# The first two tiles of a mixture-of-experts kernel taken from fixed rows, loaded while attention still runs

## What is computed

```
h  = layernorm(x)
theta, phi, g = projections of ctx, h, h to 128 channels
p  = softmax(theta @ phi)                      # 512 x 512, per batch
t  = p @ g;  t = relu(layernorm over both axes (t) * gamma + beta)
x  = x + out_w @ t + out_b + ctx               # attention
n  = layernorm(x);  w = softmax(n @ gate_w.T)  # 32 experts
w  = the 8 largest of w per token, divided by their sum
x  = x + sum over the 8 experts e of w[e] * (silu(n @ w_gate[e]) * (n @ w_up[e])) @ w_down[e]
```

## Time and profile before

| what | us |
|---|---|
| median of 3 runs | 759.28 |
| lowest, highest | 755.08, 759.33 |
| span of the profiled execution | 758.7 |

### The profile page before, as it was taken

One profiled execution on the slowest core, in us unless ns is written; L12 is line 12 of the kernel. 1 busy time (PEld: TensorE's weight loads), 2 busy tenths in 40 slices (PEclk: granted clock), 3 DMA queues, 4 the chain that ended last, 5 costly groups with the idle time before them and its releaser, 6 DMA issues.

```text
span 758.7 us, 24265 instructions
## 1 busy us (share of the span) xinstructions
PE 708.8 (93%) x3682; PEld 584.4 (77%) x3683; DVE 566.7 (75%) x1355; ACT 434.8 (57%) x1047; POOL 380.1 (50%) x297
## 2 busy tenths in 40 slices
PE   7999999988788799999999999999999999999994
PEld 5466555656667688889988999889988889888993
DVE  4578888878655488677877878877887778767882
ACT  1775666662035366556666666666667566656662
POOL 2006777767776434443544544434553455444554
PEclk9999999999799999999999999999999999999997
DMA  8996777587898999999999999999999999999995
GB/s 297 361 335 234 261 269 288 215 289 273 291 299 188 184 211 224 218 202 237 215 225 240 225 211 238 224 251 228 244 236 245 211 229 248 243 210 227 220 155 79
DMA packets 174405, 179.85 MB, mean 237 GB/s; under 512 B 36864, under 2 KB 128768, under 8 KB 174368
## 3 DMA queue, kind: packets, MB, share of 16 engines
q0 software_dynamic: 30976, 73.48, 43.0%
q1 hardware_dynamic: 118240, 67.67, 35.1%
q10 hardware_dynamic: 25152, 38.30, 15.6%
HBM read 92.25 MB, written 87.13 MB: 236 GB/s over the span
## 4 chain that ended last, share of the span: by engine, by line
SPq 38%; PE 23%; issue 18%; DMA 7%; POOL 7%; ACT 4%; DVE 2%; ACTq 1%; DVEq 1%; POOLq 0%
SPq L320 23%; SPq L325 8%; POOL x_sorted L512 6%; SPq L439 5%; PE bank L1532 3%; PE bank L1533 3%; PE bank L1539 3%; DMA x_sorted<-xn_kept,slots 3%; DMA x_all<-x_sorted 2%; PE bank L1325 2%; DMA x_sorted<-prob,last_slots 1%; PE bank L1504 1%; ACT prob L670 1%; PE bank L1505 1%; PE bank L1506 1%
## 5 line engine op out<-in xcount | busy, mean ns | idle before, releaser
L569 POOL DMA_INDIRECT out_dram<-ctx_all,x_all x144 | 243.2, 1689 | 276.7 <-issue 131.5
L1532 PE MATMUL bank<-gu_hi,xT_hi 128*128 x576 | 194.7, 338 | 2.1 <-ACT xT_hi L800 1.2
L1533 PE MATMUL bank<-gu_lo,xT_hi 128*128 x576 | 195.6, 340 | 0.0
L813 ACT ACTIVATE ctx_all<-bank 128x512 f32<-128x512 f32 x144 | 86.0, 597 | 104.9 <-issue 78.9
L512 POOL DMA_INDIRECT x_sorted<-xn_kept,slots x96 | 100.0, 1042 | 86.7 <-issue 82.0
L1539 PE MATMUL bank<-gu_hi,xT_lo 128*128 x576 | 137.9, 361 | 0.0
L1208 DVE STREAM_TRANSPOSE x_all<-x_all 128x512 f32<-128x512 f32 x146 | 103.9, 712 | 26.5 <-DMA x_all<-x_sorted 22.2
L1255 DVE SCALAR_TENSOR_TENSOR probT<-probT,x_all,bank 128x192 f32<-128x192 f32 x144 | 59.5, 413 | 79.3 <-ACT probT L821 70.5
L1532 PEld LDWEIGHTS bank<-gu_hi,xT_hi 128*128 128x128 f32 x576 | 108.5, 188 | 10.7 <-issue 5.0
L1533 PEld LDWEIGHTS bank<-gu_lo,xT_hi 128*128 128x128 f32 x576 | 108.4, 188 | 5.6
L800 ACT ACTIVATE xT_hi<-x_all 128x512 fp32r<-128x512 f32 x146 | 91.7, 628 | 34.7 <-DVE x_all L1208 34.6
(11 more groups left out here) (222 smaller groups left out, 1109.7 us busy)
## 6 DMA issues: line engine op xcount, KB each, us to landing
x_all<-x_sorted SPq DMA_DIRECT2D x578, 64.0 KB
gu_raw<-in_w_gate_up_dram ACTq DMA_DIRECT2D x28, 768.0 KB
down_raw<-in_w_down_dram ACTq DMA_DIRECT2D x28, 512.0 KB
x_sorted<-pad_rows SPq DMA_DIRECT2D x1, 8720.0 KB, 31.3
x_all<-in_x_dram SPq DMA_DIRECT2D x8, 512.0 KB, 4.9
ctx_all<-in_ctx_dram SPq DMA_DIRECT2D x8, 512.0 KB, 6.6
out_dram<-x_all SPq DMA_DIRECT2D x8, 512.0 KB, 5.9
gu_raw<-in_w_gate_up_dram SPq DMA_DIRECT2D x4, 768.0 KB
```

The lines of the kernel that those rows point to most:

```text
L569: pool.indirect_dma_start(out=out, out_offset=bass.IndirectOffsetOnAxis(ap=xw[:, k, E:E + 1].bitcast(I32), axis=0), in_=y_sb[:, i, :], in_ ...
L813: act_e.activation(y_sb[:, i, :], bank[6 + i % 2][:], ACT.Copy).then_inc(S["y_evac"], 1)
L1532: pe.matmul(out_gu, xT_hi[:, s, c * P:(c + 1) * P], gate_up(gu_hi, c), start=(c == 0), stop=False)
L1533: pe.matmul(out_gu, xT_hi[:, s, c * P:(c + 1) * P], gate_up(gu_lo, c), start=False, stop=False)
```

## The change

The first two tiles become fixed rows: rows 128 to 383 of `x_sorted`, the first 256 tokens of expert 0. Expert 0's tiles now start at its first token and not at an offset that depends on the count, and the rows behind its last token must be padding. In parts:

- SP writes padding over 256 rows of expert 0's region per batch (`pad_first_region`, 8 DMAs), and POOL waits for the fill of batch b before it scatters batch b.
- SP loads tiles 0 and 1 between `store_rows(NB - 2)` and `store_rows(NB - 1)`, when five batches are scattered and the places of batch 5 are known. `fixed_need` is 1 where expert 0 has 256 rows by then, else 2, and then SP waits for column 7 of all batches.
- Expert 0 has at least two tiles; the first row of its tiles is fixed.
- ACT shares the loads of tiles 2 and 3 with SP, no longer those of 0 to 2.
- Transposes, splits and products of tiles 0 and 1 stand between the instructions that make the tables, on DVE, ACT and PE. The small products of the tables go to banks 0 and 1. `WARM_FIRST` is one run of 12 matmuls in place of 28, 38 and 10.
- `add_tile` of tiles 0 and 1 doesn't read `first_tile` but waits for the adds before it.

```diff
-    WARM, WARM_OUT, WARM_FIRST = 20, 10, (28, 38, 10)
-    SHARED = 3
+    WARM, WARM_OUT, WARM_FIRST = 20, 10, 12
+    SHARED = 2, 3
+    FIXED = 2
...
+            def pad_first_region(b):
+
+                if type(b) is not int or b > 0:
+                    sp.wait_ge(S["first_region_padded"], 16 * b)
+                sp.dma_start(x_sorted[bass.ds(P + U * P * b, U * P), :].rearrange("(u p) h -> p u h", p=P),
+                             pad_rows[:].rearrange("p (a h) -> p a h", a=1).to_broadcast([P, U, RW])).then_inc(S["first_region_padded"], 16)
...
             load_early(2)
-            with sp.Fori(NB - 2, NB) as b:
-                store_rows(b)
+            store_rows(NB - 2)
+            pad_first_region(NB - 1)
+
+            found_need, need_fixed = (sp.alloc_register(n) for n in ("found_need", "need_fixed"))
+            for u in range(U):
+                sp.wait_ge(S[f"scattered{u}"], 16 * TOPK * (NB - 3))
+            sp.wait_ge(S["rows_stored"], 16 * (NB - 1))
+            sp.wait_ge(S["xn2_ready"], U * (NB - 2))
+            sp.wait_ge(S["fixed_rows"], 1)
+            sp.reg_load(found_need, fixed_need[0:1, 0:1])
+            sp.reg_alu(need_fixed, found_need, 1, ALU.max)
+            sp.wait_ge(S["fixed_rows"], sp.snap(need_fixed, min_val=1, max_val=2))
+            for k in range(FIXED):
+                load_x_part(sp, fixed_rows(k), k, range(HC))
+                load_xw(sp, fixed_rows(k), k, k)
+
+            store_rows(NB - 1)
             load_early(3)
...
-                pool.reg_load(first_reg, first_tile[0:1, bass.ds(j, 1)])
-                with pool.If(pool.snap(first_reg, min_val=0, max_val=1) > 0):
+                def others_added():
+
                     wait_apart(pool, "pool_passed", *((added[n], 16 * q + 16 * (n < i)) for n in range(4)))
+
+                if type(sixteen) is int and k < FIXED:
+                    others_added()
+                else:
+                    pool.reg_load(first_reg, first_tile[0:1, bass.ds(j, 1)])
+                    with pool.If(pool.snap(first_reg, min_val=0, max_val=1) > 0):
+                        others_added()
...
-            for to, value in ((experts_reg[0], 1), (half_reg[0], 0)):
-                pe.reg_mov(to, value)
+            for k in range(FIXED):
+                pe.reg_mov(experts_reg[k], 1)
+                pe.reg_mov(half_reg[k], 0)
+            pe.wait_ge(S["cum_ready"], 1)
+            ffn(0, 0)
+            pe.wait_ge(S["past_ready"], 2)
+            pe.wait_ge(S["first_row_ready"], 2)
```

More of the change, by code:

```diff
@@ L436, in read_row @@
             def read_row(eight, k):
-                if is_before(eight, k, 1) or not is_before(eight, k, EARLY):
+                if not is_before(eight, k, EARLY):
                     sp.reg_load(row_reg, x_row[0:1, bass.ds(SLOTS * eight + k, 1)])
@@ L450, in load_tile @@
                 rows = x_sorted[bass.ds(row, P), :]
-                if is_before(eight, k, SHARED):
+                if type(eight) is int and SLOTS * eight + k in SHARED:
                     load_x_part(sp, rows, i, range(HC // 2))
-                    if k:
-                        load_xw(sp, rows, i, k)
+                    load_xw(sp, rows, i, k)
                     return
@@ L835, in _ @@
             act_e.reg_mov(down_raw_reg, 4)
-            for k in range(2):
+            for k in range(FIXED):
                 xT_hi_part(k, k)
+            gate(0, 0)
+            act_e.wait_ge(S["turns_ready"], 3)
+            turns = load_turns(act_e)
+            last = load_last_turn(act_e)
+            act_e.wait_ge(S["pad_zeroed"], 32)
+            for u in range(U):
+                act_e.wait_ge(S[f"scattered{u}"], 16 * (TOPK * (NB - 1) - LATE[u]))
+            act_e.wait_ge(last_scattered[TOPK - 1], column_count(TOPK - 1))
+            act_e.wait_ge(S["rows_stored"], 16 * (NB + 1))
+            act_e.wait_ge(S["early_ready"], 1)
+            for k in SHARED:
+                load_shared(k)
+            split_act_hi(0, 0)
+            gate(1, 1)
+            xT_hi_part(2, 0)
+            xT_hi_part(3, 1)
             act_e.wait_ge(S["tables_ready"], 1)
@@ L1266, in _ @@
             dve.reg_mov(down_done_reg, 2)
-            transpose_x(0, 0)
-            xT_lo_part(0, 0)
-            transpose_x(0, 1)
-            xT_lo_part(1, 1)
+            split_act_lo(0, 0)
+            gate_product(1, 1, xw[:, 1, 0:1])
+            for k in range(2, 4):
+                transpose_x(0, k)
+                xT_lo_part(k, k % 2)
             run_quarters(dve, turns, ffn)
@@ L1533, in ffn @@
                     pe.matmul(out_gu, xT_hi[:, s, c * P:(c + 1) * P], gate_up(gu_lo, c), start=False, stop=False)
-                read_next_expert(j, (k + 1) % 4)
+                if not is_before(eight, k, FIXED - 1):
+                    if is_before(eight, k, FIXED):
+                        pe.wait_ge(S["rows_ready"], 2)
+                    read_next_expert(j, (k + 1) % 4)
                 if not is_before(eight, k, 1):
@@ L1542, in ffn @@
                     down(j - 2, (k - 2) % 4, is_before(eight, k, 4))
-            for to, value in ((experts_reg[0], 1), (half_reg[0], 0)):
-                pe.reg_mov(to, value)
+            for k in range(FIXED):
+                pe.reg_mov(experts_reg[k], 1)
[4 more added lines that the diff above has]
+            pe.wait_ge(S["first_row_ready"], 2)
+            pe.matmul(bank[0][0:1, 0:NTX], first_row[:], owned[:], start=True, stop=False)
+            pe.matmul(bank[0][0:1, 0:NTX], spare_col[:], past[:], start=False, stop=True).then_inc(S["row_done"], 1)
+            pe.wait_ge(S["cum_ready"], 3)
+            pe.matmul(bank[1][0:1, 0:NTX], ones_col[:], past[:], start=True, stop=True)
+            pe.matmul(bank[1][0:1, NTX:2 * NTX], n_tile[:], past[:], start=True, stop=True).then_inc(S["owner_done"], 1)
+            ffn(0, 1)
+            keep_clock(WARM_FIRST)
             pe.wait_ge(S["turns_ready"], 3)
```

158 lines of the change are left out of this document (76 added, 82 removed).

## The result

| | before | after |
|---|---|---|
| median of 4 runs | 758.79 us | 768.04 us (767.04 to 770.1) |
| ratio | | 1.0128, 95% interval 1.0092 to 1.0164 |
| span of the profiled execution | 758.7 us | 766.9 us |
| mean granted clock | 0.984 | 0.97 |

The changed kernel is slower, by 9.3 us between the medians; the forecast was 6.0, and 768.04 lies inside its range. The kernel was measured once more beside the later experiments, with 12 runs against 35 of before: 765.44 us (760.26 to 771.05) against 759.05, ratio 1.0083 [1.0052, 1.0113]. That is 6.4 us. Both intervals leave out 1, and they overlap. Some executions of a kernel run in a slower state: a ratio and its interval leave those out, while a time in us is the median of all executions, and where the two give different sizes both are given.

What follows compares the result with a forecast made beforehand. Though PE was 93% busy, the prediction took tile 10's load, held by POOL's late column 0 scatters, to set the end. Terms 0 + 0 + 0 + 5.5 + 0.5 = +6.0 us gave 765.3 us; range 757 to 770.

Steps and rivals of the forecast that it cites:

- The wait: On POOL, add 1 waits until add 0 has landed, delaying column 0's scatters and tile 10's load: +5.5 us.
- rival C: On POOL, the add lands as fast as a scatter: delay 3.1 us, sum 3.6, 762.9 us; 19%.
- The padding: Eight fills of expert 0's region in the attention phase slow scatters in flight, little reaching PE: +0.5 us, bounds 0 and 15.7.
- rival D: In the attention phase, fills and fixed loads cost half their bound: +13.4 us in all, 772.7 us; 15%.
- The lead: Tile 2 starts 6.4 us sooner after early tiles 0 and 1, but the wait for column 0 takes it back: 0.
- The tables: DVE makes the tables at most 4 us later, covered by at least 8 us until the new gate: cost 0.
- The steps: Forecast times at the phase change: add 1 at 236.1 us, tile 10 loaded from 248.5, PE resuming near 258.
- signs of failure: No idle between adds 0 and 1, tile 10 loaded by 243 us, first add after 231, or cadence outside 3.5-3.6 us.

Runs made afterwards that it cites:

- before_fills_2: The kernel before plus only the eight fills of expert 0's region and POOL's waits for them: 763.18 us against 759.95, ratio 1.0044.
- after_again: The changed kernel, unaltered, measured once more beside later runs of the kernel before: 765.44 us, ratio 1.0083.
- after_early18: The changed kernel, its added wait kept, with loads of tiles 10 to 17 moved ahead of the wait for column 0: 757.61 us, ratio 0.9956.
- before_early18: The kernel before with loads of tiles 10 to 17 moved ahead of the wait for column 0: 756.03 us, ratio 0.9954.
- before_wait: The kernel before with only the wait added, add 1 waiting until add 0 has landed, on a slower chip: 837.76 us, ratio 1.0072.

## Why the prediction was right, step by step

It was right in sign, in its main mechanism and, by 12 runs, in size: 765.3 us forecast, 765.44 measured. The 768.04 of the first four runs lies 2.7 above it, within the range. The terms did not fare alike: that the sum came so near is in part luck, two errors that cancel.

**The wait, +5.5 forecast: 4.3 in the traces, 5.0 (1.5 to 8.5) in the time.** The place and the path were right: "Behind it on POOL stand exactly the four scatters of column 0, and behind those SP with tile 10, DVE, and PE"; the pair with and without the gate shows it. By the traces the size was 1.2 us too high; the times cannot tell 4.3 from 5.5. I chose between add 4's wait and the later ones because the DMA engines stood at 1.03 in 228 to 236 us. While add 1 of the changed kernel waited, from 231 to 237 us, they stood at 0.75. Add 4's 4.77 was the nearer row after all: 4.57 and 4.58 in two profiles of the changed kernel. The rival C, that an add lands as fast as a scatter, is half right: by the chain it landed 5.26 - 1.62 = 3.6 us after its issue's end, against 3.4 for the scatter. But 0.9 us more pass until POOL's next DMA starts, and C left them out. The trace disagrees with the Trainium skill's fit in "DMA: Bandwidth & Descriptors", section "Anatomy of one DMA — SWDGE (gpsimd) path": its 2.6 us stand against 5.26 from issue to landing.

**The padding, +0.5 forecast: about 3 (0.5 to 6).** This is the term that was mis-sized. I saw that scatters in flight beside a fill can suffer, and let the row of PE, busy 58.49 of 60 us, cover it. A PE that is busy for 97% of a window can still be late at every half batch, if the recurring chain goes through the scatters' landing; the chain in order of time has that piece, 6.19 us at 69.96 in the kernel before, and I read it only around 230 us. The rule that I named beside it, the Trainium skill's "DMA: Bandwidth & Descriptors", section "Issuing engines are not separate DMA queues", says that transfers of all issuing engines interleave on the same 16 DMA engines. Here the trace agrees with it: landings of 6.2 us became 7.4, ScalarE's and DVE's waits for them 7.7 and 5.0 us in place of 4.5 and 6.8 (12.7 in place of 11.3 together), and two chips gave the ratios 1.0046 and 1.0044. That POOL itself does not wait for a fill was right: its first scatter starts at 60.53 us in the kernel after and at 60.42 in the kernel before. Half the bound (rival D) was too much, although D's own sign, a first load over 7 us late, did come on one chip: 211.44 in before_fills_2 against 203.46 in the earlier trace rows. The end was 3.2 us later all the same.

**The lead, 0 forecast.** The wait for column 0 took it back, as forecast: PE's wait grew by more than its restart moved, as shown above. But tile 2 did not start at 210.5 us as forecast; it started at 215.40. SP's first load behind the tables came 2.9 us later than in the earlier trace rows, and from there to the matmul 9.1 us passed in place of 6.9. Had the lead been worth something, the forecast would have been some 5 us off. With the wait removed, 1.3 us remain over before by the ratio while the fills alone cost 3.3: so some 2 us may be a gain from the lead, but each number is uncertain by some 3 us, and I leave that open.

**The clock, no term.** The changed kernel has 64 fewer of the matmuls without use, and I gave that no price. The granted clock in 200 to 220 us was 0.77 in the first profile of the changed kernel and 0.59 in after_again, against 0.96 in the kernel before. Since PE had to wait for tile 10 in any case, up to there this can have cost nothing; no run has the old number of these matmuls in the changed kernel.

**The tables, 0 forecast.** I bounded the new work among them by 4 us. They took 12.7 us (197.81 to 210.47) in place of 9.2, so 3.5 longer, of which 2.54 are the wait for PE in the first DVE row above, and began 3.2 us later. Nothing waited for them that the gate did not cover, since POOL was late in itself: right.

**The steps.** Add 1 at 236.1 (237.09), last scatter of column 0 issued at 241.9 (242.94) and landed at 246.9 (247.73), tile 10 loaded from 248.5 (249.27), PE near 258 (257.99). The wait was 1.2 us shorter than assumed and the phase began 2.2 later. One of my signs of failure was a first add after 231 us, for a loss in the attention phase; it came at 230.90, and 2.2 of the 6.3 us were lost there all the same. I had set that sign so that it only caught rival D.

**Not settled.** before_fills_2 had its phase change over 6 us late and ended 3.2 us late in the median. And after_early18, with the fills, has the ratio 0.9956, before_early18, without them, 0.9954, on two chips. Either the price of the fills is paid at the same gate as the wait's, or the lead of the fixed tiles, which tile 10 no longer takes back, pays for it: tile 10's load came at the same time in both, though the first load was 8.6 us late. No run has the fills and the moved loads without the fixed tiles, so the two are not told apart. In the front part I gave the lines of SP's wait for all columns as 458 to 460; the wait is in the loop a few lines further down.

## What to carry to other kernels

When a wait is put on an in-order queue, its price is not the wait but what stands behind it in the queue, and who holds the next gate: a wait of 4.6 us cost 5.0 us (1.5 to 8.5) with the gate behind it, and nothing that could be measured without it, though there it was 5.2 us long. A gate that asks for more than the consumer needs (tile 10 waited for a column that it cannot contain) turns every delay on the producer's side into time; moving eight loads ahead of it gave 3.0 us, while putting the gate's own scatters first gave 1.1, which is not clear of the noise. And cover is read from the chain in order of time in the stretch where the edit acts, not from a busy share: a busy engine says nothing of whether the transfer beside it is on the recurring chain.

## What the runs showed of the hardware

Chips differed more than kernels did here: the same kernel before took 833.16 us on one chip and 759.05 and 759.95 on two others, and nearly all of it lies ahead of tile 10's load (at 315.93 us in before_wait, 73 us later than in the earlier trace rows). There the DMA engines were less busy, not more (0.56 against 0.80 at 60 to 120 us). And a fill of 545 KB, whose data take some 2 us of all engines by the large fill's rate, took 9.7 us from issue to landing in the median of eight, among other transfers; the one large fill of 8720 KB took 32.4. An add that had to wait for the one before it sat 4.2 to 5.2 us on POOL at the start of the tiles (4.57 at a DMA share of 0.75), and 6.7 to 7.2 us in the middle of the kernel, at 1.03.
